# Mixture-of-experts stage: gathered token rows turned by transposing transfers instead of TensorE

## The reference, cut to what matters

```python
g = jnp.einsum('th,eih->tei', x, dyn_gate_w)        # x: layer-normed tokens, e: 8 experts, i: 256
u = jnp.einsum('th,eih->tei', x, dyn_up_w)
y_dyn = jnp.einsum('tei,ehi->teh', jax.nn.silu(g) * u, dyn_down_w)
out = jnp.einsum('te,teh->th', global_w[:, :E_DYN], y_dyn)
gs = jnp.einsum('th,fih->tfi', x, sh_gate_w)        # the shared expert, i: 1024
us = jnp.einsum('th,fih->tfi', x, sh_up_w)
out = out + jnp.einsum('tf,tfh->th', global_w[:, E_DYN:], jnp.einsum('tfi,fhi->tfh', jax.nn.silu(gs) * us, sh_down_w))
```

## Time and profile before

| | us |
|---|---|
| median of 3 runs | 1261.3 (1254.98 to 1262.98) |
| the profiled execution, its time | 1259.68 |
| its span, first to last instruction | 1257.9 |
| TensorE busy in the span | 1204.5 |
| VectorE, ScalarE, GpSimd busy | 952.3, 709.4, 582.2 |
| mean granted TensorE clock (share of 2.4 GHz) | 0.991 |

### The profile page before, as it was taken

The page is one execution under the profiler, slowest core; times in us unless marked ns, Lnnn a source line. Parts: engine busy times, 40 slices in busy tenths (PEclk is TensorE's granted clock), DMA queues, the critical chain, the costliest instruction groups (busy, mean ns, idle before and its releaser), DMA issues.

```text
span 1257.9 us, 29768 instructions
## 1 busy us (share of the span) xinstructions
PE 1204.5 (96%) x10916; PEld 838.5 (67%) x10916; DVE 952.3 (76%) x2006; ACT 709.4 (56%) x1988; POOL 582.2 (46%) x685
## 2 busy tenths in 40 slices
PE   6888998889999999999999999999999999999996
PEld 3555655678888888886444444777777777666663
DVE  5899898799999998887677777777777775645451
ACT  4377787699999998896344222222222231555553
POOL 0047678537667776732300000777776100355624
PEclk9999999899999999999999999999999999999999
DMA  9522023133545454553890051222223510687846
GB/s 346 210 68 69 1 33 45 43 94 131 169 144 173 161 162 149 165 165 115 169 209 1 10 159 34 69 35 69 48 55 87 200 68 1 218 174 204 188 55 84
DMA packets 132224, 144.01 MB, mean 114 GB/s; under 512 B 53200, under 2 KB 86128, under 8 KB 132080
## 3 DMA queue, kind: packets, MB, share of 16 engines
q1 hardware_dynamic: 114240, 119.65, 32.1%
q0 software_dynamic: 13248, 21.15, 9.3%
q10 hardware_dynamic: 4592, 1.32, 0.5%
HBM read 84.93 MB, written 57.19 MB: 113 GB/s over the span
## 4 chain that ended last, share of the span: by engine, by line
PE 86%; DVE 7%; issue 2%; DMA 2%; ACT 2%; POOL 1%; SPq 0%; DVEq 0%; POOLq 0%; ACTq 0%
PE bank L121 31%; PE bank L2126 15%; PE bank L2119 13%; PE bank L1503 6%; PE bank L1435 4%; PE bank L955 4%; PE bank L1456 3%; PE bank L1450 3%; PE bank L1421 2%; PE bank L1024 2%; PE bank L2405 1%; PE bank L872 1%; DMA q_rows<-att_land 1%; PE bank L961 1%; PE bank L891 1%
## 5 line engine op out<-in xcount | busy, mean ns | idle before, releaser
L1624 POOL DMA_INDIRECT lists<-att_land x128 | 133.1, 1040 | 208.8 <-DVE att_land L1764 167.4
L1353 ACT ACTIVATE att_land<-bank,att_land 128x120 f32<-128x120 f32 x512 | 178.3, 375 | 15.5 <-DVE att_land L1221 15.4
L2119 PE MATMUL bank<-att_land 128*128 128x512 f16 x768 | 176.2, 379 | 0.6 <-DVE program_logits L1304 0.6
L1946 ACT ACTIVATE att_land<-program_x 128x512 f32<-128x512 f32 x40 | 25.2, 631 | 195.1 <-DVE program_x L2088 195.1
L2119 PEld LDWEIGHTS bank<-att_land 128*128 128x128 f16 x768 | 75.0, 98 | 82.1 <-issue 0.6
L121 PE MATMUL bank<-program_xs,program_wgu 128*128 128x512 f16 x576 | 128.7, 379 | 0.6 <-DVE att_land L1723 0.6
L121 PE MATMUL bank<-att_land 128*128 128x128 f16 (+2 forms) x1944 | 113.5, 212 | 1.0 <-issue 0.5
L1353 ACT ACTIVATION_READ_ACCUMULATOR att_land<-bank,att_land 128x1 f32 x512 | 112.9, 221 | 0.0
L121 PEld LDWEIGHTS bank<-att_land 128*128 128x128 f16 x1944 | 105.3, 98 | 5.9 <-issue 1.3
L1785 POOL DMA_INDIRECT att_land<-xn_rows,att_land x40 | 39.1, 978 | 143.2 <-DMA out_rows<-att_land 98.9
L121 PEld LDWEIGHTS bank<-program_xs,program_wgu 128*128 128x128 f16 x576 | 56.2, 98 | 67.6 <-DVE att_land L1723 1.1
(11 more groups left out here) (299 smaller groups left out, 2827.2 us busy)
## 6 DMA issues: line engine op xcount, KB each, us to landing
att_land<-q_rows SPq DMA_DIRECT2D x96, 128.0 KB, 2.6
xn_rows<-att_land SPq DMA_DIRECT2D x37, 256.0 KB, 3.9
out_rows<-att_land SPq DMA_DIRECT2D x37, 256.0 KB, 2.5
q_rows<-att_land SPq DMA_DIRECT2D x32, 256.0 KB, 2.9
xt_tiles<-att_land SPq DMA_DIRECT2D x32, 256.0 KB, 2.1
x_rows<-program_x SPq DMA_DIRECT2D x8, 1024.0 KB, 4.6
att_land<-x_rows SPq DMA_DIRECT2D x8, 1024.0 KB, 5.8
program_xs<-xt_tiles SPq DMA_DIRECT2D x28, 256.0 KB, 5.0
```

Of the source, the lines that this page charges most:

```text
L1353: last = act.activation(prob[:, c, h, :], ps_s[c % 2][:, h, :], ACT.Exp, bias=nmax[:, u % 2, c, h:h + 1], accum_out=rsum[:, u % 2, n:n + 1])
L1624: pool.indirect_dma_start(out=io["lists"], out_offset=bass.IndirectOffsetOnAxis(ap=index[:, t, k:k + 1], axis=0), in_=load[:, t, k, :], in ...
L2119: last = pe.matmul(ps_y[i][:, :], hid[:, c % 2, a, i * P:(i + 1) * P], wd[:, q, c, :], start=c == 0 and n == 0, stop=c == NC - 1 and n == 2)
```

## The change

1. The PE transposes of gathered rows, `rows_transposed`, are gone, and with them the banks `ps_x` and the semaphores `xt_mm`, `xt_hi`, `xt_lo`.
2. `rows_high` and `rows_low` now split a gathered tile as it lies: ScalarE writes the f16 high half and VectorE the low half of `xg[:, c, n]` (SBUF, token rows on partitions) into one of four slots of `halves`, 2 x 512 f16 for each partition. They stand at the same places of their engines' orders as before. They wait for the gather itself (`x_in`) and for the slot to have been turned.
3. SyncE issues, for each tile, one `dma_start_transpose` from the slot (128 partitions by 1024 f16) into `xT` (8 blocks of 128 by 128, SBUF to SBUF). It waits for both halves, and for the transfer before the last one to have landed. These five stand behind `expert_weights(e + 2)` in SyncE's step.
4. TensorE's `unit(e, 0)` and `unit(e, 2)` wait for these transfers (3 tiles, 5 tiles) instead of for VectorE.
5. The next gather waits for VectorE's `row_lo` instead of the transposes.
6. `xT` is two tensors at other places, so that expert 0's tiles may be split and turned during chunks 3 to 7 of the last batch of the shared expert; the shared stage yields for them there and no longer among its last down products.

```diff
 def shared(...):  # sync
         for b in range(B + 1):
             step(b)
-            yield
+            yield "rows" if b == B - 1 else None
...
                     # scalar, vector (the same edit in both)
-        yield "rows"
+            if b == B - 1 and c >= NC - CT:
+                yield "rows"
...
                     # vector
         low(B * NC - 1)
-        for n in range(3):
-            yield "rows"
         rows(B - 1, range(TB))
...
                     # tensor
         for v in range(B * NC - 2, B * NC):
-            yield "rows"
-            yield "rows"
             down(v)
...
 def experts(g, io, sem, banks, f):
+    SLOTS = 4
-    xT = g.old(6 * D, [P, 2, 2, KC, CAP], f16)
+    xT = [g.old(at * D, [P, 2, KC, CAP], f16) for at in (16, 11)]
+    halves = g.xs[:, 0].rearrange("p q k n -> p (q k n)").rearrange("p (s q n) -> p s q n", s=SLOTS, q=2)
-    hid = g.old(16 * D, [P, 2, 2, NI, CAP], f16)
-    ps_x = [b[:, :].rearrange("p (k n) -> p k n", k=KC) for b in banks[0:2]]
+    hid = g.old(6 * D, [P, 2, 2, NI, CAP], f16)
+    turned = [sem() for n in range(2)]
...
+    def tiles_turned(eng, tiles):
+
+        for n in range(2):
+            need(eng, turned[n], 16 * ((tiles + 1 - n) // 2))
+
     def sync(sp):
+        def rows_turned(u, c, n):
+            t = CT * u + n
+            need(sp, s["row_hi"], t + 1)
+            need(sp, s["row_lo"], t + 1)
+            need(sp, turned[t % 2], 16 * (t // 2))
+            if n == 0:
+                need(sp, s["u_mm"], 4 * (u - 1))
+            sp.dma_start_transpose(xT[c][:, :, :, n * P:(n + 1) * P].rearrange("p q k n -> p (q k) n"),
+                                   halves[:, t % SLOTS].rearrange("p q n -> p (q n)")).then_inc(turned[t % 2].handle, 16)
+
         def step(e, d):
             u = e + 2
             if ok(u):
                 need(sp, s["w_hi"], 3 * (u - 2))
                 need(sp, s["w_lo"], 3 * (u - 2))
                 expert_weights(sp, g, io, u, d % 2)
+            u = e + 1
+            if ok(u):
+                for n in range(CT):
+                    rows_turned(u, (d + 1) % 2, n)
+        need(sp, f.products, f.all_products - 7 * (IS // P))
+        for n in range(CT):
+            rows_turned(0, 0, n)
+        yield
         need(sp, f.w0_hi, 3)
         need(sp, f.w0_lo, 3)
-        for e in range(E - 2):
+        for e in range(E):
             step(e, e % 2)
...
     def gpsimd(pool):
-                need(pool, s["xt_mm"], CT * (u - 1))
+                need(pool, s["row_lo"], CT * (u - 1))
                 gather_rows(pool, g, io, u)
...
         def rows_high(u, c, n):
-            need(act, s["xt_mm"], CT * u + n + 1)
+            t = CT * u + n
             if n == 0:
-                need(act, s["u_mm"], 4 * (u - 1))
-            act.activation(xT[:, c, 0, :, n * P:(n + 1) * P], ps_x[n % 2][:, :, :], ACT.Copy).then_inc(s["xt_hi"].handle, 1)
+                need(act, x_in[c], 16 * CT * (u // 2 + 1))
+            tiles_turned(act, t + 1 - SLOTS)
+            act.activation(halves[:, t % SLOTS, 0], xg[:, c, n], ACT.Copy).then_inc(s["row_hi"].handle, 1)
...
         def rows_low(u, c, n):
-            need(dve, s["xt_hi"], CT * u + n + 1)
-            cols = slice(n * P, (n + 1) * P)
-            dve.tensor_tensor(xT[:, c, 1, :, cols], ps_x[n % 2][:, :, :], xT[:, c, 0, :, cols],
-                              ALU.subtract).then_inc(s["xt_lo"].handle, 1)
+            t = CT * u + n
+            need(dve, s["row_hi"], t + 1)
+            if n == 0:
+                need(dve, x_in[c], 16 * CT * (u // 2 + 1))
+            tiles_turned(dve, t + 1 - SLOTS)
+            dve.tensor_tensor(halves[:, t % SLOTS, 1], xg[:, c, n], halves[:, t % SLOTS, 0],
+                              ALU.subtract).then_inc(s["row_lo"].handle, 1)
...
     def tensor(pe):
-                    need(pe, s["xt_lo"], CT * u + (3 if h == 0 else CT))
+                    tiles_turned(pe, CT * u + (3 if h == 0 else CT))
...
-        def rows_transposed(u, c, n):
-            if n == 0:
-                need(pe, x_in[c], 16 * CT * (u // 2 + 1))
-            if u == 0 and n == 0:
-                need(pe, f.mix, f.mixed - 2)
-            need(pe, s["xt_lo"], CT * u + max(n - 1, 0))
-            for k in range(KC):
-                last = pe.transpose(ps_x[n % 2][:, k, :], xg[:, c, n, k * P:(k + 1) * P], g.ident[:, :])
-            last.then_inc(s["xt_mm"].handle, 1)
...
-                if ok(e + 1):
-                    rows_transposed(e + 1, after, n)
-                    if n == 3:
-                        rows_transposed(e + 1, after, 4)
```

More of the change, by code:

```diff
@@ L2205, in shared @@
     done.w0_hi, done.w0_lo, done.mix, done.y_ok = (s[n] for n in ("w0_hi", "w0_lo", "mix", "y_ok"))
-    done.mixed = 7 * (B * NC - SEVEN)
+    done.mixed = done.all_products = 7 * (B * NC - SEVEN)
+    done.products = s["prod"]
     return done
@@ L2214, in experts @@
     w = [g.ex_w0, g.old(0, [P, 2, WN], f16)]
-    xT = g.old(6 * D, [P, 2, 2, KC, CAP], f16)
+    xT = [g.old(at * D, [P, 2, KC, CAP], f16) for at in (16, 11)]
+    halves = g.xs[:, 0].rearrange("p q k n -> p (q k n)").rearrange("p (s q n) -> p s q n", s=SLOTS, q=2)
     sg = g.land(0, [P, 2, HN])
     hf = g.land(2 * HN, [P, 2, HN])
-    hid = g.old(16 * D, [P, 2, 2, NI, CAP], f16)
-    ps_x = [b[:, :].rearrange("p (k n) -> p k n", k=KC) for b in banks[0:2]]
+    hid = g.old(6 * D, [P, 2, 2, NI, CAP], f16)
     ps_g, ps_u = ([banks[k][:, 0:HN] for k in pair] for pair in ((2, 4), (3, 5)))
     ps_y = banks[6:8]
-    s = {n: sem() for n in ("w_hi", "w_lo", "xt_mm", "xt_hi", "xt_lo", "g_mm", "u_mm", "silu", "hf", "h_hi", "h_lo",
+    s = {n: sem() for n in ("w_hi", "w_lo", "row_hi", "row_lo", "g_mm", "u_mm", "silu", "hf", "h_hi", "h_lo",
                                "y_mm", "y_ok")}
     s["added"] = g.ex_added
+    turned = [sem() for n in range(2)]
     w_in, x_in = g.ex_w_in, g.ex_x_in
@@ L2391, in unit @@
                 if n % 2 == 0 and at == 0:
-                    need(pe, s["xt_lo"], CT * u + (3 if h == 0 else CT))
+                    tiles_turned(pe, CT * u + (3 if h == 0 else CT))
                 matmuls(pe, bank[n % 2][:, :],
                         lambda a, k: w[c][:, a, at + k * IE + i * P:at + k * IE + (i + 1) * P],
-                        lambda a, k: xT[:, c, a, k, h * HN:(h + 1) * HN]).then_inc(s[sem].handle, 1)
-        def rows_transposed(u, c, n):
-            if n == 0:
-                need(pe, x_in[c], 16 * CT * (u // 2 + 1))
-            if u == 0 and n == 0:
-                need(pe, f.mix, f.mixed - 2)
-            need(pe, s["xt_lo"], CT * u + max(n - 1, 0))
-            for k in range(KC):
-                last = pe.transpose(ps_x[n % 2][:, k, :], xg[:, c, n, k * P:(k + 1) * P], g.ident[:, :])
-            last.then_inc(s["xt_mm"].handle, 1)
+                        lambda a, k: xT[c][:, a, k, h * HN:(h + 1) * HN]).then_inc(s[sem].handle, 1)
         def step(e, d):
@@ L2432, in step @@
                         outputs(u, after, i)
-        for n in range(CT):
-            rows_transposed(0, 0, n)
-            yield
         for e in range(E + 1):
```

## The result

| | before | after |
|---|---|---|
| median, range | 1259.9 us (1255.0 to 1263.0) | 1287.8 us (1286.0 to 1288.0) |
| profiled span, mean granted clock | 1257.9 us, 0.991 | 1285.9 us, 0.980 |
| start of the first expert product | 1076.66 us | 1075.32 us |
| from there to the start of TensorE's last block of outputs | 168.07 us | 197.31 us |

The changed kernel is slower: ratio 1.022, 95% interval 1.020 to 1.024. The first expert product starts 1.34 us earlier: the transposes ahead of it held 2.4 us (0.88, 1.09 and 0.44), the new wait and its restart take 0.9 back, and the shared stage was 0.2 us late.

The account below looks back on a forecast made before the run. TensorE's instructions were taken to bound the experts' part, without a gap. Removed transposes less one wait (-16.9 us) plus seven stalls of 2.5 us (+17.5) gave +0.6 us, a median of 1262 us; range 1252 to 1290 us.

Parts of the forecast that it names:

- what is removed: TensorE's fp32 transposes of gathered rows: 40 tiles at 0.44 us each, 17.5 us gained.
- the one wait in the shared expert: Before the shared expert's last down product TensorE waits 0.64 us for VectorE's low half, leaving 16.9 us net gain.
- the walk: From unit 2's issue to the next expert: tile 2 split at +2.7 us, landing 3.0 us, stall 2.5 us in seven experts.
- Rival 4: A transfer's eight blocks go one behind another, holding every expert: 1354 us or more; chance 0.06.
- rival 3: Tile 2 isn't late for the next expert's first unit: all 16.9 us are kept, 1244 us; chance 0.09.
- the price of a transfer on the DMA engines: One 256 KB transposing transfer keeps the DMA engines busy for 1.4 us, taken from loads in small pieces.
- rival 2: Transposing transfers are slow or fill the DMA engines, 25.4 us of work an expert: 1276 or 1290 us; chance 0.25.
- The paragraph on the collision: Tile 2 leaves at 21.5 us after unit 3's end, when the five adds (issued to +19.2) are just through.
- with the clock held: Main forecast, 0.42: stalls of 1.6 to 2.9 us without the granted clock falling behind them, 1256 to 1265 us.
- rival 1: Granted clock falls behind TensorE's stalls, 1.7 us each; in all seven +12 us more, 1274 us; chance 0.18.
- 0.40 for slower: Chance of over 1% slower, summed from three rivals' shares: 0.09 + 0.25 + 0.06.
- weights behind transfers in SyncE's queue: Named as a way to be wrong: TensorE waits for weights that now come behind the transfers; no size given.

Follow-up runs that it names:

- e2: Changed kernel without the accumulating adds into the output (which then lacks the routed experts); median +9.5 us against the kernel before, one run.
- e10: Hybrid: tiles 0 to 2 of experts 2 to 7 and all of expert 0 by transfers, the rest by TensorE; +7.8 us against the kernel before.
- e12: Kernel before plus 35 unread transposing transfers, with weights of expert e + 3 ahead of those of tiles 2 to 4 in SyncE's order; +14.4 us.
- e6: Changed kernel without the weight loads of experts 2 to 7; median +13.7 us against the kernel before, one run.
- e7: Kernel before, with its TensorE transposes, plus 35 transposing transfers that nobody reads, one in flight at a time; +24.2 us.
- e1: Changed kernel with tiles 1 to 3 split sooner, so that tile 2 has two units to land; +15.2 us against the kernel before.
- e4_after: Changed kernel again, unaltered, on the slow chip; +22.7 us against the kernel before.
- e8: Kernel before, unaltered, run for its trace; 168.06 us from the first expert product to the start of TensorE's last block of outputs.
- e11: Changed kernel without the accumulating adds and with 22 filler transposes behind unit 3 of the first seven experts; -2.2 us against the kernel before, one run.

## Why the prediction was right or wrong

The forecast was 1262 us, which is no change. 1287.8 us were measured, 27.9 us above the median before.

**Right: what is removed.** The transposes' 17.5 us, and the one wait in the shared expert: 0.7 us measured, 0.64 forecast.

**Right: where TensorE waits, and the walk.** Seven waits, all for tile 2, ahead of the first matmul of an expert; three of the seven lie in the 1.6 to 2.9 us forecast. Where the transfer was undisturbed the wait is 2.54, 2.56, 2.42 us for a forecast 2.5. Six waits of e2 say the same. That it came out to a tenth is luck: for the 2.54 us the transfer left 2.4 us after unit 3's start, not 2.7, and from there to TensorE's start it was 3.4 us, not 3.0 (3.1 for the landing, 0.25 until TensorE started). Rival 4 is out: all eight blocks landed within 3.0 to 3.2 us. So is rival 3: no tile 2 was in time.

**Right: the price of a transfer on the DMA engines.** 1.4 us from the earlier trace rows, 1.4 measured. By the 261 GB/s that the Trainium skill (DMA: Bandwidth & Descriptors, Latency and other measured facts) gives, the estimate would have been 1.0 us; the trace has 1.4. The sum for rival 2, 25.4 us of work an expert, is right for the shorter periods, 25.9 and 25.6 us (1.08 x 23.94, 1.07 x 23.97), and too low for the longer ones, 31.3 and 34.3 us (1.15 x 27.26, 1.19 x 28.82). By the windows these moved some 9% more bytes in some 27% more busy time: in the crowd the packets themselves took longer.

**Wrong: the step that weighed rival 2.** The sum was right and was then argued away: "gathers, weights and adds each have over 10 us of slack, which takes up most of a lag". Its own numbers say otherwise: a lag of 3.4 us in each of some five experts is 17 us, and each had been given a slack of over 10. And the transfers themselves are in the crowd. The paragraph on the collision had the adds "just through" when tile 2 leaves, some 2 us behind the last issue; at 1139 us they still held 69% of the engines 3 us behind it. The landing that stood in seven terms of the sum as 3.0 us was 4.7 to 6.6 us for tile 2 of the hard-hit experts, and twice tile 2 was held before it left, for 2.5 and 1.9 us longer than the usual 0.06, by a tile 0 that took 9.0 and 14.9 us. Undisturbed, the waits would be 7 x 2.5 = 17.5 us; they were 30.6. The term is short by 13.1 us: some 4.4 us of it are the two holds, the rest tile 2's own landings.

**Wrong: "with the clock held".** It fell behind all seven, from 2.42 us of standing still up, and cost 12.8 us in all; rival 1 had it at 12 us and had been given 0.18. The row at 252 us on which I leaned had TensorE idle in pieces, not for 2.5 us at a stretch. The length of a wait alone doesn't decide it. In the experts of all runs the clock held behind the waits of up to 1.97 us and fell behind those of 3.2 us and more. Between them it did now the one, now the other: it fell behind 2.12 us (e2), 2.14 (e10) and 2.42 (the changed kernel), and held behind 2.19 us (e12), 2.56 (e6) and 2.86 (e10). Two timeline lines show it, of e2_noadds and e10_three_tiles; at the full clock the 18 matmuls of the first take 4.05 us and the 24 of the second 3.42:

```profile
1330.99 5.73 PE L121 MATMUL bank<-att_land,program_x 128*128 128x512 f16 x18 [2.12 <-ACT program_x L2310]
...
1137.66 3.42 PE L121 MATMUL bank<-program_x 128*128 128x320 f16 x24 [2.86 <-DMA program_x<-program_xs]
```

**So** rivals 1 and 2 both came true, and I had priced them as alternatives: the forecast with both their amounts, +12 and +14 us, would have been 1288 us. They measured 12.8 and 13.1. The range, to 1290, held the time by luck: rival 2's far bound reached there for a reason of its own, a landing of 7 us for every tile 2. The sign has the same root: 0.40 for slower was made of cases added side by side, where each makes the other likelier (late landings lengthen the waits, and behind every long wait the clock fell).

**Named beforehand and seen only in the experiments:** weights behind transfers in SyncE's queue. In the changed kernel they left 4.9 to 9.2 us after their buffer was free (experts 3 to 7) and TensorE never waited for them; in e7 all but 0.8 us of what TensorE waited more was for ScalarE, and ScalarE waited 23.3 us for weights.

**Open.** How much of the 13.1 us would be left if no transfer waited for another: taking the holds off might only move the landings. Why it is mostly every other expert that is hit: after a short wait the period is short (24 us) and leaves work over, after a long one (27 to 29 us) it is cleared; this fits the rows and wasn't tested.

## What to carry to other kernels

Before moving work from an engine to the DMA engines, multiply their share by the period and add the new work: where the sum exceeds by much the period that you hope for, expect the transfers to land late however much slack each had. Here 25.4 us for 22.0 and 22.6 for 20.4 (three tiles of five) brought waits, 21.2 for 20.8 (two tiles) did not, so a little over is not yet a loss. A transfer that something waits for belongs where nothing else is in flight, and nothing that is needed soon should stand behind it in a queue that waits for landings. A wait that is short but ends TensorE's run of work is to be priced with the clock that may fall behind it: here 2.42 us of standing still cost 4.3 (the last block's 22.66 us for 20.82 on top).

## What the runs showed of the hardware that I had not expected

A transposing transfer of 256 KB inside SBUF lands in 3.0 to 3.2 us alone and in up to 14.9 us beside gathers, weights and adds, while the DMA engines' share goes only from 0.85 before the change to between 1.0 and 1.2: landings grow far more than shares tell.

On the chip of e1 to e7 and e12 TensorE, VectorE and ScalarE stood still for long stretches while GpSimd issued the small indirect transfers of the lists; for most of them the records name no releaser. All eight profiles from there have them. The kernel before has none from there, but its medians are as much longer. The windows of e4_after, one such stretch (columns as above):

```profile
900.00:925.00 25.00, 0.00 (x0) 0.00 (x0) 0.00 (x0) 0.00 (x0) 19.21 (x20) 0.50 0.02 1
```

TensorE's longest in e1_early was 48.7 us. Its standstills of over 3 us add up to 142 to 148 us in each of the eight profiles, and the kernels take some 180 us longer. The profiles of the first runs and of e8 to e11 have none. Its cause is open.
